# One wait for two quads of gathers in a graph network's attention loop

## The reference

```
q, k, v = projections of the normalised nodes
att = einsum('ehd,ehd->eh', q[dst], k[src]) / 4, clipped
alpha = softmax of att over the edges with the same dst
aggr = segment_sum(v[src] * alpha, dst)
x = x + (aggr @ Wo + bo)
x = x + gelu(layernorm(x) @ W1 + b1) @ W2 + b2
```

## Time and profile before

| | us |
|---|---|
| median of 3 runs | 3509.81 |
| lowest and highest run | 3503.63, 3520.41 |
| span of the profiled execution | 3472.7 |
| PE busy | 2377.0 (68%) |
| DVE busy | 1981.1 (57%) |
| ACT busy | 1704.5 (49%) |
| POOL busy | 1820.8 (52%) |

### The profile page before, as it was taken

How to read it: one execution, slowest core, us unless ns; L and a number is a source line. 1 busy time by engine, 2 the same in 40 slices (tenths; PEclk the granted TensorE clock), 3 DMA queues, 4 the chain that set the end, 5 groups by cost and what they waited for, 6 DMA issues and landing times.

```text
span 3472.7 us, 60241 instructions
## 1 busy us (share of the span) xinstructions
PE 2377.0 (68%) x13853; PEld 2027.0 (58%) x13854; DVE 1981.1 (57%) x7060; ACT 1704.5 (49%) x4472; POOL 1820.8 (52%) x1968
## 2 busy tenths in 40 slices
PE   6998774567667676777667746666666666666667
PEld 6988333556556565656556635556565565565556
DVE  7887782455555555555556625555555455554555
ACT  6765653345445444545445434354444445454444
POOL 5642655655555555555555245556555555555552
PEclk9999885778878878878888867788778778787788
DMA  7865232222322222222223122222222222222221
GB/s 211 242 207 172 88 106 85 85 77 84 89 86 84 84 79 85 79 86 82 82 83 88 45 72 83 82 81 84 81 77 78 81 79 81 77 81 81 78 84 37
DMA packets 180176, 323.48 MB, mean 93 GB/s; under 512 B 38740, under 2 KB 93991, under 8 KB 179892
## 3 DMA queue, kind: packets, MB, share of 16 engines
q0 software_dynamic: 80208, 216.22, 21.7%
q1 hardware_dynamic: 98948, 103.44, 9.7%
q10 hardware_dynamic: 736, 0.93, 0.1%
HBM read 288.09 MB, written 20.71 MB: 89 GB/s over the span
## 4 chain that ended last, share of the span: by engine, by line
another core or an unknown queue 15%; PE 13%; issue 10%; DVE 8%; DVEq 3%; ACT 3%; ACTq 0%; DMA 0%; SPq 0%
PE bank L2080 5%; DVE aggregate L2120 3%; PE bank L2071 2%; PE bank L1729 2%; PE bank L1723 1%; DVE arena L2128 1%; ACT arena L2013 1%; PE bank L2056 1%; PE bank L1720 1%; DVE arena L2148 1%; DVEq L2109 1%; DVE arena L2162 1%; DVEq L2120 1%; PE bank L1718 1%
## 5 line engine op out<-in xcount | busy, mean ns | idle before, releaser
L1992 POOL DMA_INDIRECT arena<-kv_rows,idx_stage x1612 | 1540.8, 956 | 1344.6 <-DVE arena L2128 798.4
L2080 PE MATMUL bank<-arena 128*128 128x136 f32 x3328 | 698.7, 359 | 654.1 <-DVE aggregate L2120 551.8
L2120 DVE TENSOR_TENSOR aggregate<-bank,aggregate 128x136 f32 x1664 | 493.9, 297 | 1017.6 <-remote 851.3
L2080 PEld LDWEIGHTS bank<-arena 128*128 128x128 f32 x3328 | 589.1, 249 | 746.1 <-DVE aggregate L2120 419.9
L2071 PE MATMUL bank<-queries,arena 128*128 x3328 | 547.5, 317 | 82.0 <-DVE arena L2148 53.6
L2071 PEld LDWEIGHTS bank<-queries,arena 128*128 128x128 f32 x3328 | 509.9, 233 | 91.3 <-issue 90.8
L2013 ACT ACTIVATE arena<-iota_n,at_negdst 128x128 f32<-128x128 f32 x1664 | 527.7, 395 | 3.8 <-DMA kv_rows<-arena 2.0
L1777 ACT ACTIVATE arena<-bank 128x256 f32<-128x256 f32 (+1 forms) x225 | 85.0, 379 | 731.8 <-remote 454.8
L2056 PE MATMUL bank<-ident,arena 128*128 128x128 f32 x1664 | 325.7, 329 | 106.1 <-issue 63.0
L2148 DVE TENSOR_TENSOR arena<-bank,arena 128x512 f32<-128x512 f32 x416 | 284.6, 684 | 152.8 <-remote 68.2
L2037 ACT ACTIVATE arena<-arena 128x32 f32<-128x32 f32 x416 | 92.8, 223 | 556.0 <-DVE arena L2177 336.3
(11 more groups left out here) (322 smaller groups left out, 2796.3 us busy)
## 6 DMA issues: line engine op xcount, KB each, us to landing
arena<-in_edge_attr_dram SPq DMA_DIRECT2D x244, 256.0 KB
arena<-kv_rows,idx_stage POOLq DMA_INDIRECT x1612
kv_rows<-arena SPq DMA_DIRECT2D x12, 512.0 KB, 3.8
kv_rows<-arena SPq DMA_DIRECT2D x24, 256.0 KB, 2.2
arena<-in_x_dram SPq DMA_DIRECT2D x12, 256.0 KB, 4.0
x_rows<-arena SPq DMA_DIRECT2D x12, 256.0 KB, 2.9
x_stream<-arena SPq DMA_DIRECT2D x12, 256.0 KB, 2.3
queries<-arena SPq DMA_DIRECT2D x12, 256.0 KB, 2.7
```

Source lines behind the costliest of these rows:

```text
L1992: pool.indirect_dma_start(kv[:, n, :], None, kv_dram[l], bass.IndirectOffsetOnAxis(idx_stage[:, half % 2, n:n + 1], 0)).then_inc(Z.kv_in[s ...
L2080: pe.matmul(sums_of(j), sel[:, r % SEL_SLOTS, j, :], msg[:, r % 2, j, :], start=True, stop=True).then_inc(Z.sum, 1)
L2120: dve.tensor_tensor(a, sums_of(j), a, ALU.add).then_inc(Z.added, 1)
```

## The change

Before, POOL waits before each quad k for message k-8. In the change it waits only before an even r, and there for message k-7, which is the message for the slots of quad k+1. The gathers of both quads then follow without a wait between them. In the first body the first eight quads have no wait in both kernels. Nothing else is changed: the wait for indices stays, and the instructions of PE, DVE, ACT and SP are the same in the same order.

```
                 for r in range(QUADS):
                     slot = r % (KV_QUADS)
                     k = i * QUADS + r
-                    if not (first and r < KV_QUADS):
-
-                        pool.wait_ge(Z.msg, k0 + k - KV_QUADS + 1)
+                    if r % 2 == 0 and not (first and r < KV_QUADS):
+
+                        pool.wait_ge(Z.msg, k0 + k - KV_QUADS + 2)
                     half = r * QUAD // KV_SLOTS
                     if slot == 0:
                         pool.wait_ge(Z.idx, (k0 // QUADS + i) * HALVES + half + 1)
```

## The result

The change takes 3568.49 us (median of 4 runs, 3561.55 to 3577.01), the kernel before, in runs taken beside it, 3515.11 (3503.63 to 3522.84). The ratio is 1.0158, with a 95% interval of 1.0138 to 1.0179: slower, by more than twice the +0.7% of the forecast, and inside its range.

The account below looks back on a forecast made before the run. It took PE's signals, held back while POOL's gathers follow without a gap, as the bound. Terms of 0 and +25 us for the starting message, added to the median 3509.81, gave 3535 us, range 3488 to 3609.

Parts of the forecast that it names:

- What bounds the kernel: POOL's unbroken gathers delay what PE makes known, released 2.6 us after a run's last gather begins; 13.9 us per two quads.
- The lead: Gathers start later, but some 40 us are left against 5 us to issue, so L2148 does not wait: 0 us.
- The waits that go: 200 of POOL's 400 waits and their register steps vanish, hidden by POOL's idle time: 0 us.
- Which message starts a run: In steady bodies all POOL runs start on odd messages: +2.2 us a body in layer 1, +0.6 in layer 2, +25 total.
- The first bodies: First four bodies of each layer, where updates begin and no pattern shows: 0 us, bounds of 18 us either way.
- The later bodies: The 9 bodies with full updates in each layer: 9 x 2.2 + 9 x 0.6 = 25 us.
- Begin and end of a layer: Second run 5.0 us earlier at the start, PE's signals 5.0 us later at the end: 0 in each layer.
- The pair slips: Rival: POOL waits 3.82 us longer for a pair's second message; one slip a body costs 99 us, 3609; chance 0.23.
- From the span to the time: The median of before is 37.1 us above the profiled span of 3472.7; the forecast adds 25 to that median.
- Nothing moves: Rival: POOL already does runs of 8, and late releases are unrelated to gathers or phases cost the same: 3510; chance 0.20.
- fewer starts: Rival: POOL has 8 starts a body in place of 9, saving time: 3445 to 3490 us; chance 0.12.

Follow-up runs that it names:

- e16: Kernel before with only the 32 gathers that fill the ring in each layer, the rest left out: 2436.69 us against 3530.98.
- e9: Kernel before with half of each quad's gathers left out after the first eight quads of a layer: 2466.62 us against 3478.61.
- e17: Kernel before with POOL also waiting, ahead of each quad, until the previous quad's gathers have landed; second kind of chip: 3693.26 us against 3530.98.
- e18: Kernel before, unchanged, run for its trace on a chip of the first kind, where it takes 2696 to 2703 us.
- e6: Kernel before with one wait per four quads, for four messages, on the first kind of chip: 2697.86 us, ratio 0.9999.
- e5: The change itself again, beside the kernel before, on the first kind of chip: 2700.76 us, ratio 1.0003.
- e13: The change with pairs beginning at odd quads, so runs start on even messages; second kind: 3585.8 us against 3511.6 for the kernel before, ratio 1.0206.
- e14: Kernel before with each quad's wait for one message more (k-7 for k-8), no grouping; second kind: 3521.94 us against 3511.6, ratio 1.0033.
- e15: Kernel before with one wait per four quads, for four messages, on the second kind of chip: 4000.88 us against 3530.98, ratio 1.1335.
- e10: The change itself again, beside the kernel before, on the second kind of chip: 3550.38 us against 3478.61, ratio 1.0205.
- e2: Kernel before with POOL also waiting, ahead of each quad, until the previous quad's gathers have landed; first kind of chip: 3692.28 us, ratio 1.3665.

## Why the prediction was off

*What bounds the kernel: right, for one kind of chip.* That unbroken gathers delay what PE makes known was an inference. e16, e9 and e17 bear it out on the second kind: without gathers, with half of them, or with a break after each quad the "remote" time of L2120 is gone. The Trainium skill's rule that DMA doesn't contend with a compute engine ("SBUF — State Buffer", "Who interferes with whom"), taken as the prediction took it, describes the first kind (L2120 idles 111.2 us in e18) and not the second (1017.6 us, and 139.9 without gathers). Contention for the memory itself is shown by no run here; what is late are increments. The other caution, that a matmul's end in the profile is estimated ("Perfetto Trace Analysis", "Tensor Engine Instruction (MATMUL, LD_WEIGHTS)"), doesn't account for the wait either: the same estimates stand in e16 and e17, where it is gone.

A count over the traces, which no view groups, fits. PE's recorded increments for the products of L2080, each paired with the last modelled end before it, come over 1 us late in 47% of cases before, 51% in the change, 7% in e17, 3% in e9, and under 1% in e16 and e18. The traces lack some of the increments' records (128 of 1664 before, 493 in e17); paired from the product's side, with the next record, the shares are 46, 52, 20, 13 and under 1%. Before, a product that PE issues during the first gather of a run is seldom late, during the second in about one case of six, and from the fourth on nearly always. It is PE alone: each of its four semaphores in the layers has 35 to 65% late, while of the recorded increments of DVE and ACT under 1% are.

*The lead: right.* L2148 idles 161.9 us against 152.8, and e6 shows that twice the grouping is free as well where nothing else counts.

*The waits that go: right.* e5 has them gone too, at a ratio of 1.0003.

*Which message starts a run (+25): not the main term.* A typical steady body is nearly as worked out (115.45 for 114.26, 110.39 for 109.82). But e13, which starts all its runs on the other messages, costs as much as the change, and e14, which has the delay and part of the phase without the pairs, costs 10 to 12 us.

**The step that failed** is that the sum prices the phase alone and puts the need for both messages at nothing: 0 for the first bodies, 0 for slips, and no longer runs. The runs show the reverse. Of the change's 53 us the need for both messages is some 40, going by e14 (which was on another chip, and in mixed phase); in the other phase (e13) the pairs cost 74 us; with groups of four (e15) the cost is 470.

*The first bodies (0 +- 18): wrong.* This is where the pair's price shows most plainly. The three bodies from quad 8 to quad 56 of layer 1, by DVE's comparison of L2171, before:

```profile
627.20 0.18 DVE L2171 TENSOR_TENSOR arena<-arena 128x32 f32<-128x32 f32 x1
...
943.50 0.18 DVE L2171 TENSOR_TENSOR arena<-arena 128x32 f32<-128x32 f32 x1
```

After:

```profile
631.94 0.18 DVE L2171 TENSOR_TENSOR arena<-arena 128x32 f32<-128x32 f32 x1
...
963.39 0.18 DVE L2171 TENSOR_TENSOR arena<-arena 128x32 f32<-128x32 f32 x1
```

They went from 316.3 to 331.5 us, those of layer 2 from 311.0 to 335.4: 40 us, by the two traces. The other traces agree: 333.7 and 332.9 in e10, the change on another chip, and 317.3 and 315.6 in e14, which has no pairs. I had looked for a pattern only where one was plain to see.

*The later bodies.* Over the nine bodies from quad 56 to quad 200 of both layers the change's trace is 68 us longer than that of before, e10's 47, where the forecast had 25. But e14's is 46 us longer too, and its kernel is only 10 to 12 us slower than before on the same chip. So part of this is the trace of before. It took about 3474.5 us with the 1.8 added. On the chip of e9 and e10 the kernel before takes 3477 to 3482; on the other chips of the second kind none of its 22 runs is under 3497. That trace may thus be of a chip like e10's rather than of a lucky execution; nothing on record decides it, and no second trace of before on the second kind exists.

*Begin and end of a layer (-5 + 5): small, with the parts off.* POOL's second run comes 4.9 and 5.4 us sooner, as forecast, but quad 8 reaches L2171 only 1.5 and 0.9 us sooner. Behind quad 200 the layers are 4 and 5 us shorter, where the forecast had 5 longer.

*The pair slips: the rival that was there.* Its price was nearly right (3.82 us for a step; 17.51 in place of 13.9 in the one shown, 18.36 in the mean of 8). There are 8 such steps in the change and none before. Its total was worked out for one in each body, 26, and the sum had none. Beside them stand the 13 runs of 13 to 16 gathers, which neither the forecast nor a rival had: when both messages come early enough the next pair follows without a gap, PE's signals stay away for 16 gathers, and the gap behind is 9 us. An estimate by these counts: 197 gathers in such runs at 1.80 us instead of the 1.65 of the runs of 12 that before has in their place, some 30 us; eight slips at 4.4 (18.36 less 13.94), 35. With the 12 of e14 that is 77, and the medians say 53 and, on the chip of e10, 72. The split is not shown: e13 costs 74 us with only 3 slips and 7 of the longer runs in its trace.

*From the span to the time: wrong.* Time less span is 1.8 us in the profile of the change and 1.7 to 2.1 in those of the experiments. I took the 37.1 for an offset. It did no harm to the sum, which had only to be a difference, but it hid that the profile was no typical run.

*Nothing moves and fewer starts.* The first holds exactly on the first kind of chip (1.0003). The second fell: 184 waits for messages in place of 254, and POOL idle for longer.

**What stays open** is why some chips hold PE's signals back while POOL issues gathers and others don't. Nothing that the profile shows names it, and no run tells POOL's issuing of the gathers from the moving of their data. e2 and e17 give 3692 and 3693 us, so a gather and its landing take the same on both kinds; the part ahead of the layers too takes some 540 us on both. A break shorter than a full landing after each quad, which could be the remedy on the second kind, wasn't tried. No complete kernel here is faster than the one before on either kind.

## What to carry to other kernels

A wait that asks for a group is as late as the group's last member, and costs when the waiting engine starts just behind such a member; grouping waits is free only where the engine never reaches them unfulfilled, so look at how often each wait is a real one (here 254 times against none) before anything else. Where a loop settles into a repeating pattern, price the change also on the bodies that are not yet in it, and ask whether the profiled run is a typical one. If the profile has long waits whose releaser it can't name, run the unchanged kernel on a second chip before reasoning about them.

## What the runs showed of the hardware

- The same kernel takes 2696 to 2703 us in the median on three chips and 3479 to 3531 on at least three others. Two of the first three were met more than once, and were of the first kind each time. Whether it is the chip or something around it can't be told from here.
- On the second kind PE's semaphore increments come late while POOL issues indirect DMAs of 128 rows of 1 KB without a gap (DVE's longest wait for them is 14.8 us in the change, and about half are over 1 us late). With runs of four and a landing wait between them (e17) 7 to 20% are, by how the records are paired. In the two places shown, the wait ends 2.6 and 2.8 us after the last gather begins.
- PE's mean granted clock is 0.93 to 0.95 of full speed in most kernels on the first kind and 0.80 to 0.81 in the change on the second. It goes with the waiting and not with the kind of chip: e16 on the second kind has 0.94, and e2 on the first 0.79.
- One such gather costs POOL 1.25 us from one to the next, and 3.5 from the last of a quad to the next quad where POOL waits for its landing.
